# Latent attention: a list-scheduled order, masks of the maxima added by TensorE, single rows of maxima

## The chip, the cores and the metric

One core of one Trainium2 chip runs the kernel. The metric is the device time of the whole program in microseconds (us); the median of three runs of the kernel before is 1757.98 us. TensorE multiplies matrices into PSUM, VectorE (DVE) and ScalarE (ACT) read PSUM, GpSimd (POOL) works on SBUF alone, SyncE (SP) starts transfers.

## What is computed

A block of six layers over 2048 rows of 128 features: an expert layer with eight experts, windowed attention, the expert layer again, then a latent-attention block with four experts, a state-space layer, and the latent-attention block again. The change is in the latent attention, of which this is the core (16 heads of size 8, here over T = 2048 rows):

```python
scores = jnp.einsum('bhqd,bhkd->bhqk', q, k) / np.sqrt(HEAD_DIM)
causal = jnp.tril(jnp.ones((t, t), dtype=bool))
scores = jnp.where(causal, scores, -jnp.inf)
attn = jax.nn.softmax(scores, axis=-1)
out = jnp.einsum('bhqk,bhkd->bhqd', attn, v).transpose(0, 2, 1, 3).reshape(b, t, D_MODEL)
return out @ Wo.T
```

## The kernel before

`latent_attention` works in 16 units a stage, each of one group g of 512 query rows (four tiles of 128) and four heads; `ORDER` runs g = 0, 0, 1, 1, 2, 2, 3, 3, 3, 3, 2, 2, 1, 1, 0, 0. A unit has two passes.

The pass of maxima finds each query row's largest score. For each query tile, head and block of up to 512 keys, one item ("max", numbered m): TensorE puts 128 rows of scores into one of three PSUM banks (`maximum`, L1592; the contraction has 64 rows, so that two heads use the two row halves of the array), and VectorE takes the maximum over the columns. A unit has 16(g+1) items. Blocks left of the diagonal go through `tensor_reduce` (L1761). The block on the diagonal, 128 to 512 columns wide, needs the causal mask: `tensor_tensor_reduce` (L1766) adds the table `causal` (in SBUF, 512 columns of bf16) and reduces, and writes its sums to `masked`. At a unit's end VectorE joins the blocks' maxima (L1772) into `shift`, waits for that, and GpSimd (`chain_shift`, L1804 to L1807) writes it in three bf16 parts beside the queries, so that the second pass's scores come out less their maxima.

The pass of scores takes key tile after key tile (4(g+1) tiles, two halves of two heads each): TensorE makes transposed scores into a pair of banks (`score`, L1602, two pairs in turn), ScalarE takes the exponential of up to 1024 columns (L1709), GpSimd zeroes what lies above the diagonal in a unit's first four tiles (`cut_products`, L1826), and TensorE multiplies with the values (`weigh`, L1618, f32; a tile is weighed in two halves of 256 query rows). `plain` and `shift` are transposes of the unit's queries without and with the maxima (L1580) and their copies on ScalarE (L1714). `take` (L1734) and `out` (L1628, L1777, L1779) bring a unit's result back into rows. Beside them stand the output projection, the norm and routing of half of the rows (`mean`, `root`, `norm`, `turn`, `logits`, `place`; after `place` GpSimd issues eight indirect transfers, L545), in the first stage also 64 exponentials `power` (L1742) and four products `times_c` for the state-space layer.

All engines follow one list, `events`, made by `plan` before the program is built; each engine takes its own kinds of event from it, in order, and waits on semaphores. Before, a place is a number: item m of unit v stands at its index, the scores of a unit are spread evenly over the next unit's items behind a lead of 9, and everything else is set by an offset to these. Maxima stand in pairs, and TensorE waits once for both banks of a pair:

```python
if m % 2 == 0:
    bank_free(("max", (v, m + 1)))
```

## Time and profile before

| | us |
|---|---|
| median of three runs | 1757.98 |
| lowest, highest | 1755.60, 1759.52 |
| profiled execution | 1757.22 |
| its span | 1755.9 |
| busy: PE, DVE, ACT, POOL | 1238.1, 1196.7, 947.0, 570.0 |
| mean granted clock of TensorE, share of full | 0.834 |

A span is the time from the first to the last instruction. Busy time counts what an engine executes, not its waits; ends of matmuls are modelled. A row of the order of time gives the start, how long the instructions lasted, engine, line, operation, what is written and read with shapes (64*128 means 64 rows by 128 columns of the array), the count, and in brackets the idle time before it and what ended that. Neighbouring instructions overlap, so the distance from start to start is what one costs its engine. The clock is TensorE's, 1.00 for 2.4 GHz and 0.50 for 1.2 GHz.

### The profile page before, as it was taken

What the parts mean: (1) busy time and instruction counts of PE and PEld (TensorE: products, weight loads), DVE (VectorE), ACT (ScalarE), POOL (GpSimd) and SP (SyncE); (2) the same over time, 40 slices, a digit from 0 to 9 for tenths busy, and PEclk for the clock granted to TensorE, in tenths of its full rate; (3) what the DMA queues carried; (4) which work ended last, traced back from release to release, by engine and by line L of the source; (5) the groups of instructions that cost most, each with busy time, mean ns of one, the idle gap of its engine ahead of it and who ended that gap; (6) DMA issues with size and microseconds to landing.
All of it is one profiled execution on the core that took longest, in us unless ns stands there. A gap on an engine that the chain in (4) does not pass through costs nothing. (4 is left out here: it accounts for less than half of the span.)

```text
span 1755.9 us, 36353 instructions
## 1 busy us (share of the span) xinstructions
PE 1238.1 (71%) x13313; PEld 624.7 (36%) x13313; DVE 1196.7 (68%) x3279; ACT 947.0 (54%) x1500; POOL 570.0 (32%) x1032
## 2 busy tenths in 40 slices
PE   2754564366757788899886464776778898988746
PEld 2653453365532122222232453353222222223246
DVE  4358598436777899987862354277789999786234
ACT  0226774122445688888875240134557788887522
POOL 2331276146662411321123242275332111112323
PEclk9977675577577999999998695856799999999869
DMA  9410000021001100000000180000000000000012
GB/s 243 102 46 1 1 4 2 22 66 50 1 18 53 35 1 1 1 2 3 1 1 13 49 217 27 2 1 1 1 1 2 1 2 1 1 2 1 13 44 81
DMA packets 59137, 49.01 MB, mean 28 GB/s; under 512 B 7105, under 2 KB 54194, under 8 KB 58610
## 3 DMA queue, kind: packets, MB, share of 16 engines
q1 hardware_dynamic: 53282, 35.84, 7.9%
q0 software_dynamic: 4736, 9.74, 1.7%
q8 instruction: 109, 1.79, 0.4%
q10 hardware_dynamic: 944, 1.10, 0.2%
q14 instruction: 66, 0.54, 0.1%
HBM read 32.72 MB, written 18.38 MB: 29 GB/s over the span
## 5 line engine op out<-in xcount | busy, mean ns | idle before, releaser
L1709 ACT ACTIVATE arena<-psum 128x1024 f32<-128x1024 f32 (+3 forms) x640 | 561.0, 898 | 191.6 <-PE psum L1602 170.8
L1761 DVE TENSOR_REDUCE arena<-psum 128x1 f32<-128x512 f32 x768 | 479.8, 683 | 63.4 <-PE psum L1592 59.7
L1618 PE MATMUL psum<-arena 128*9 128x256 f32 (+2 forms) x4352 | 346.4, 394 | 0.9 <-POOL arena L1826 0.4
L1592 PE MATMUL psum<-arena 64*128 64x512 bf16 (+3 forms) x1280 | 240.2, 371 | 128.7 <-DVE arena L1761 58.3
L1766 DVE CUSTOM_DVE_ANT_0 arena<-psum,wqkv 128x384 bf16<-128x384 f32 (+3 forms) x512 | 230.3, 486 | 89.0 <-PE psum L1592 75.1
L1602 PE MATMUL psum<-arena 64*128 64x512 bf16 (+3 forms) x1280 | 233.7, 362 | 20.0 <-ACT arena L1709 15.0
L1826 POOL TENSOR_SCALAR_AFFINE_SELECT arena<-arena 128x256 f32<-128x256 f32 x256 | 103.6, 408 | 323.0 <-ACT arena L1709 320.4
L1592 PEld LDWEIGHTS psum<-arena 64*128 64x128 bf16 x1280 | 64.0, 94 | 383.2 <-DVE arena L1761 196.6
L1618 PEld LDWEIGHTS psum<-arena 128*9 128x9 f32 x4352 | 67.7, 89 | 174.3 <-issue 133.5
L1804 POOL CAST arena<-arena 128x16 bf16<-128x16 f32 x64 | 16.4, 257 | 327.7 <-DVE arena L1772 325.4
L677 DVE TENSOR_SCALAR small<-psum,YT 128x128 f32<-128x128 f32 x168 | 50.5, 342 | 78.0 <-PE psum L587 77.4
L632 ACT ACTIVATE small<-psum,YT 128x128 f32<-128x128 f32 x168 | 52.4, 364 | 83.5 <-PE psum L587 64.6
L587 PE MATMUL psum<-arena,YT 128*128 128x128 f32 x672 | 97.1, 292 | 0.1
L1602 PEld LDWEIGHTS psum<-arena 64*128 64x128 bf16 x1280 | 63.5, 95 | 93.1 <-ACT arena L1709 46.6
L1714 ACT ACTIVATE arena<-psum 128x1024 bf16<-128x1024 bf16 x64 | 65.5, 1023 | 52.3 <-PE psum L1580 48.3
L587 PEld LDWEIGHTS psum<-arena,YT 128*128 128x128 f32 x672 | 87.6, 204 | 2.9 <-issue 1.3
L578 PE MATMUL psum<-ident,ACCn 128*128 128x128 f32 x16 | 7.2, 470 | 90.7 <-DMA ACCn<-sorted_rows 58.1
L559 POOL DMA_INDIRECT made_rows<-arena,index x38 | 42.4, 1116 | 76.8 <-DVE arena L657 75.1
L545 POOL DMA_INDIRECT sorted_rows<-Yn,slot x32 | 31.4, 980 | 83.9 <-DVE slot L363 74.8
L597 PE MATMUL psum<-w,small 128*128 x304 | 43.0, 286 | 15.7 <-ACT small L632 12.7
L1580 PE MATMUL psum<-identb,arena 128*128 128x128 bf16 x512 | 44.5, 237 | 9.9 <-DVE psum L1750 3.9
L597 PE MATMUL psum<-big_w,small 128*128 x368 | 50.5, 281 | 0.6 <-issue 0.6
(353 smaller groups left out, 1962.9 us busy)
## 6 DMA issues: line engine op xcount, KB each, us to landing
arena<-taps SPq DMA_DIRECT2D x8, 1024.0 KB
big_w<-in_w SPq DMA_DIRECT2D x2, 2048.0 KB
ACCn<-made_rows SPq DMA_DIRECT2D x16, 256.0 KB, 3.6
regions<-sorted_rows SPq DMA_DIRECT2D x5, 741.8 KB, 4.6
sorted_rows<-arena SPq DMA_DIRECT2D x2, 1483.5 KB, 16.8
ACCn<-regions SPq DMA_DIRECT2D x32, 64.5 KB, 1.9
w<-in_w SPq DMA_DIRECT2D x2, 1024.0 KB
ACCn<-sorted_rows SPq DMA_DIRECT2D x6, 258.0 KB, 3.4
```

The source lines that it names most:

```text
L587: mm = pe.matmul(hidden_of(s, k), first[s % 2][:, k * P:(k + 1) * P], xt[s // GT % 2][:, (s % GT) * P:(s % GT + 1) * P], start=True, stop= ...
L597: mm = pe.matmul(psum[:, 4 + s % 2, 0:D], hid[s % 2][:, k, :], flat2[:, bass.ds(expert[s] * HID + k * P, D)], start=(k == 0), stop=(k == H ...
L632: half = act.activation(hid[s % 2][:, k, :], hidden_of(s, k), ACT.Relu, bias=first[s % 2][:, HID + k:HID + k + 1])
L677: half = dve.tensor_scalar(hid[s % 2][:, k, :], hidden_of(s, k), first[s % 2][:, HID + k:HID + k + 1], 0.0, ALU.add, ALU.max)
L1592: pe.matmul(psum[:, b, 0:w], plain_q[v % 2][rows, a, i * P:(i + 1) * P], keys[rows, 2 * hq + a, c * GW:c * GW + w], start=True, stop=True) ...
L1602: mm = pe.matmul(psum[:, b + r, off:GW], keys[rows, 2 * hq + a, t * P:(t + 1) * P], shift_q[v % 2][rows, a, off:GW], start=True, stop=True)
L1618: mm = pe.matmul(psum[32 * hh:32 * hh + 9, O_BANK, lo:hi], values[:, tile_of(v, j), 4 * hq + hh, :], prob[(t + hh // 2) % N_PROB][:, hh % ...
L1709: act.activation(prob[t % N_PROB][:, :, off:GW], both, ACT.Exp, scale=INV_SQRT_HD).then_inc(a_got, 1)
L1714: act.activation(dst, bank.bitcast(BF16).rearrange("p (a t) -> p a t", a=2), ACT.Copy).then_inc(a_got, 1)
L1761: dve.tensor_reduce(place, bank[:, 0:w], AX.X, ALU.max).then_inc(a_max_got, 1)
L1766: dve.tensor_tensor_reduce(out=masked[cuts % 2][:, 0:w], in0=bank[:, 0:w], in1=causal[:, GW - w:GW], scale=1.0, scalar=LEAST, op0=ALU.add, ...
L1826: pool.affine_select(out=part, in_=part, compare_op=ALU.is_ge, fill=0.0, base=0, pattern=[[0, 2], [1, P]], channel_multiplier=-1).then_inc ...
```

## The change

Four things change.

The order. `plan` no longer computes places but lists: it keeps a time at which each engine is free, by a table of costs, and emits whichever event of TensorE's could start soonest, ties by a rank. Items run ahead of the scores as banks come free. Events of the other engines are put into the list when their input is ready. A tile's two half weighings stand together. `power` is put wherever ScalarE would idle, and the products `scale` follow after each sixteenth.

Single rows. TensorE waits for one bank at each item instead of two banks at each pair.

The masks. A diagonal item is a matmul of the scores with start only, followed by a second matmul of `identb` with a 128-column bf16 table `causal` that adds -1e30 above the diagonal to the last 128 columns of the bank. VectorE's custom operation, its 512-column table and the two `masked` buffers are gone; all items are `tensor_reduce` (L1921 in the changed kernel).

The joining. A unit's maxima are joined after the first item of the next unit, not at its own end, without a wait behind; `row_max` has two buffers for that.

In the diff, cut to its core, "..." marks what is left out:

```diff
-LEAST = -3e38
...
-        causal = wqkv[:, D:3 * D].bitcast(BF16)
+        causal = wqkv[:, D:D + P // 2].bitcast(BF16)
...
-            places = []
-            start = [ITEMS_TO[v + 1] + LEAD for v in range(UNITS)] + [N_ITEMS + LEAD + 4 * TILES_OF[-1]]
-            half_at = [start[v] + (start[v + 1] - start[v]) * s / (2 * TILES_OF[v]) for v in range(UNITS) for s in range(2 * TILES_OF[v])]
-            half_at += [half_at[-1] + 2 * k for k in range(1, 24)]
-            for v in range(UNITS):
-                places += [(ITEMS_TO[v] + m - m % 2, "max", (v, m)) for m in range(4 * TILES_OF[v])]
-                places += [(ITEMS_TO[v] - 8 if v else -1, "plain", v), (start[v] - 3.1, "shift", v)]
-                places += [(half_at[2 * (TILES_TO[v] + j) + a] - 0.4, "score", (v, j, a)) for j in range(TILES_OF[v]) for a in range(2)]
-                for j in range(TILES_OF[v]):
...
+            free = {e: 0.0 for e in ("pe", "dve", "act", "pool")}
+            done, act_ring, dve_ring, weighed, later = {}, [], [], [], []
...
+            def put_act(kind, x, ready, pe_cost, cost):
+                p = run("pe", ready, pe_cost) + 0.15
+                while far and at["power"] < 64 and done.get(("score", (1, 0, 0))) and free["act"] + 0.2 < p + LAG:
+                    power(p)
+                emit(kind, x)
+                done[kind, x] = run("act", p + LAG, cost)
+                act_ring.append(done[kind, x])
...
+            def joined(v):
+                done["least", v] = run("dve", done.get(("chain", v - 1), 0.0) + LAG, 0.15)
+
+                def shifted(ready):
+                    done["chain", v] = run("pool", ready, 1.6)
+                put_off(done["least", v], "chain", v, shifted)
...
+                v, m = at["item"]
+                if v < UNITS and ("plain", v) in done:
+                    ready = done["plain", v] + LAG
+                    yield max(ready, ring_free(dve_ring, 3)), 6, "max", (v, m)
+                v, h = at["half"]
+                if v < UNITS and ("shift", v) in done and len(weighed) >= TILES_TO[v] + h // 2 - 2:
+                    yield max(done["shift", v] + LAG, ring_free(act_ring, 2)), 5, "score", (v, h // 2, h % 2)
+                v, j = at["weigh"]
...
+                v, j = at["weigh"]
+                if v < UNITS and ("score", (v, j, 1)) in done and (j or not v or ("take", v - 1) in done):
+                    ready = done["score", (v, j, 1)]
+                    if j < GT:
+                        ready = done.get(("cut", (v, j, 1)), 1e9)
+                    if j == 0 and v:
+                        ready = max(ready, done["take", v - 1])
+                    yield ready + LAG, 4, "weigh", (v, j)
...
+            while True:
+                options = [(max(free["pe"], ready), *rest) for ready, *rest in choices() if ready < 1e8]
+                if not options:
+                    if not later:
+                        break
+                    flush(min(entry[0] for entry in later))
+                    continue
+                soonest = min(options)[0]
+                if any(entry[0] <= soonest for entry in later):
+                    flush(soonest)
+                    continue
+                ready, _, kind, x = min((o for o in options if o[0] <= soonest + 0.05), key=lambda o: o[1])
+                if kind in ("plain", "shift"):
...
+                    put_dve(kind, x, ready, 0.22 * w / GW + (0.1 if c == ORDER[v][0] else 0.0), 0.067 + 0.533 * w / GW)
+                    at["item"] = (v, m + 1)
+                    if m + 1 == 4 * TILES_OF[v]:
+                        at["item"] = (v + 1, 0)
+                    if m == 0 and v:
+                        joined(v - 1)
+                    if at["item"] == (UNITS, 0):
+                        joined(v)
...
+                    put_act(kind, x, ready, 0.225 * w / GW, 0.19 + 1.66 * w / 1000)
...
+                    parts = [0.225 * (min(GW, k + GW // 2) - max(k, cut(v, j))) / (GW // 2) for k in (0, GW // 2) if cut(v, j) < k + GW // 2]
+                    for half in ((1,) if j == 0 else (0, 1)):
+                        emit(kind, (v, j, half))
+                    weighed.append(run("pe", ready, sum(parts)) + 0.16)
...
-                    if m % 2 == 0:
-                        bank_free(("max", (v, m + 1)))
-                    pe.matmul(psum[:, b, 0:w], plain_q[v % 2][rows, a, i * P:(i + 1) * P],
-                              keys[rows, 2 * hq + a, c * GW:c * GW + w], start=True, stop=True).then_inc(a_max_put, 1)
+                    bank_free(event)
+                    mm = pe.matmul(psum[:, b, 0:w], plain_q[v % 2][rows, a, i * P:(i + 1) * P],
+                                   keys[rows, 2 * hq + a, c * GW:c * GW + w], start=True, stop=(c < g))
+                    if c == g:
+                        mm = pe.matmul(psum[:, b, w - P:w], identb[:], causal, start=False, stop=True)
...
+                def joined(v):
+                    dve.wait_ge(a_max_got, dve_base + number["max", (v, 4 * TILES_OF[v] - 1)] + 1)
+                    if units + v:
+                        dve.wait_ge(a_chained, units + v)
+                    dve.tensor_reduce(shift, row_max[v % 2][:, :, 0:ORDER[v][0] + 1], AX.X, ALU.max, negate=True).then_inc(a_least, 1)
+
...
-                        place = row_max[:, i * 4 + hh, part:part + 1]
-                        if part < ORDER[v][0]:
-                            dve.tensor_reduce(place, bank[:, 0:w], AX.X, ALU.max).then_inc(a_max_got, 1)
-                        else:
-                            cuts += 1
-                            if cuts > 2:
-                                dve.wait_ge(a_max_got, dve_base + number[event] - 1)
-                            dve.tensor_tensor_reduce(out=masked[cuts % 2][:, 0:w], in0=bank[:, 0:w], in1=causal[:, GW - w:GW], scale=1.0,
-                                                     scalar=LEAST, op0=ALU.add, op1=ALU.max, accum_out=place).then_inc(a_max_got, 1)
-                        if m == 4 * TILES_OF[v] - 1:
-                            dve.wait_ge(a_max_got, dve_base + number[event] + 1)
-                            if units + v:
-                                dve.wait_ge(a_chained, units + v)
-                            dve.tensor_reduce(shift, row_max[:, :, 0:ORDER[v][0] + 1], AX.X, ALU.max, negate=True).then_inc(a_least, 1)
-                            dve.wait_ge(a_least, units + v + 1)
+                        dve.tensor_reduce(row_max[v % 2][:, i * 4 + hh, part:part + 1], bank[:, 0:w], AX.X, ALU.max).then_inc(a_max_got, 1)
+                        if m == 0 and v:
+                            joined(v - 1)
+                        if (v, m) == (UNITS - 1, 4 * TILES_OF[v] - 1):
+                            joined(v)
...
+                    elif kind == "scale":
+                        times_c(x)
```

In TensorE's order, in unit 8 of the first stage (g = 3), L1592 is an item, L1602 a half of a score tile, L1618 a half weighing. Before:

```order
985 L1592 MATMUL psum<-arena 128x512 x2
986 L1602 MATMUL psum<-arena 128x512 x2
987 L1618 MATMUL psum<-arena 9x256 x4
988 L1592 MATMUL psum<-arena 128x512 x2
989 L1602 MATMUL psum<-arena 128x512 x2
990 L1618 MATMUL psum<-arena 9x256 x4
991 L1592 MATMUL psum<-arena 128x384 x2
992 L1602 MATMUL psum<-arena 128x512 x2
993 L1618 MATMUL psum<-arena 9x256 x4
```

In the changed kernel, the same unit; L1745 is an item, L1748 a mask, L1758 a half of a score tile, L1774 a weighing:

```order
1137 L1758 MATMUL psum<-arena 128x512 x2
1138 L1745 MATMUL psum<-arena 128x512 x2
1139 L1774 MATMUL psum<-arena 9x256 x8
1140 L1758 MATMUL psum<-arena 128x512 x2
1141 L1745 MATMUL psum<-arena 128x384
1142 L1748 MATMUL psum<-wqkv,identb 128x128
1143 L1758 MATMUL psum<-arena 128x512 x2
1144 L1745 MATMUL psum<-arena 128x384
1145 L1748 MATMUL psum<-wqkv,identb 128x128
1146 L1745 MATMUL psum<-arena 128x512
1147 L1774 MATMUL psum<-arena 9x256 x8
```

Where each half tile had two items, a score and a half weighing, a tile now has its items in ones and twos between the scores and is weighed at once, and each diagonal item has a 128-column matmul behind it.

On GpSimd, near the end of the first stage, L1826 zeroes above the diagonal, L1804 to L1807 write a unit's maxima, and L545 is `place`'s eight indirect transfers. Before:

```order
351 L1807 CAST arena<-arena 128x4x4
352 L1826 AFFINE_SELECT arena<-arena 128x2x128
353 L545 DMA regions<-ACCn,slot 8576x129 x8
354 L1826 AFFINE_SELECT arena<-arena 128x2x128 x4
355 L1804 CAST arena<-arena 128x4x4
356 L1805 TENSOR_TENSOR arena<-arena 128x16
357 L1804 CAST arena<-arena 128x4x4
358 L1805 TENSOR_TENSOR arena<-arena 128x16
359 L1807 CAST arena<-arena 128x4x4
360 L1826 AFFINE_SELECT arena<-arena 128x2x128 x12
361 L545 DMA regions<-ACCn,slot 8576x129 x8
```

In the changed kernel the lines are L1978, L1956 to L1959 and L544:

```order
351 L1957 TENSOR_TENSOR arena<-arena 128x16
352 L1959 CAST arena<-arena 128x4x4
353 L544 DMA regions<-ACCn,slot 8576x129 x8
354 L1956 CAST arena<-arena 128x4x4
355 L1957 TENSOR_TENSOR arena<-arena 128x16
356 L1956 CAST arena<-arena 128x4x4
357 L1957 TENSOR_TENSOR arena<-arena 128x16
358 L1959 CAST arena<-arena 128x4x4
359 L1978 AFFINE_SELECT arena<-arena 128x2x128 x24
360 L544 DMA regions<-ACCn,slot 8576x129 x8
```

Sixteen cuts, those of the last two units, stood behind the first eight transfers; now it is twenty-four, those of the last three, and the last unit's maxima are written ahead of them.

## Rows read from the trace of the kernel before

**Rows 1.** The page: the span.
```profile
span 1755.9 us, 36353 instructions
```

**Rows 2.** Stretches, first stage: length, busy PE, PEld, DVE, ACT, POOL, then clock, DMA.
```profile
496.20:517.70 21.50, 13.43 (x80) 6.13 (x82) 14.81 (x66) 7.07 (x9) 10.29 (x29) 0.55 0.00 0
517.70:663.70 146.00, 114.19 (x1090) 32.34 (x1086) 127.55 (x320) 96.20 (x142) 46.06 (x129) 0.91 0.10 32
663.70:781.70 118.00, 105.13 (x1132) 26.53 (x1128) 110.93 (x250) 100.68 (x131) 28.74 (x47) 1.00 0.01 2
781.70:900.50 118.80, 107.12 (x1262) 34.48 (x1264) 92.69 (x239) 98.28 (x123) 17.91 (x52) 1.00 0.01 2
900.50:943.80 43.30, 33.50 (x310) 11.59 (x302) 19.79 (x91) 29.83 (x43) 15.09 (x30) 0.80 0.04 13
943.80:958.00 14.20, 10.26 (x114) 4.31 (x110) 1.79 (x5) 9.63 (x22) 5.98 (x17) 1.00 0.00 1
sum 461.80, PE 383.62 PEld 115.38 DVE 367.57 ACT 341.69 POOL 124.08; mean PE 63.94 PEld 19.23 DVE 61.26 ACT 56.95 POOL 20.68
```

**Rows 3.** The same, two stretches of the second stage.
```profile
1488.50:1603.50 115.00, 103.23 (x1137) 31.12 (x1136) 92.48 (x239) 95.95 (x119) 17.92 (x52) 1.00 0.01 1
...
1645.70:1663.00 17.30, 13.69 (x126) 4.79 (x118) 1.80 (x6) 10.13 (x23) 6.36 (x18) 0.80 0.00 1
```

**Rows 4.** The page, groups: busy, mean ns, idle before and who ended it.
```profile
L1761 DVE TENSOR_REDUCE arena<-psum 128x1 f32<-128x512 f32 x768 | 479.8, 683 | 63.4 <-PE psum L1592 59.7
...
L1766 DVE CUSTOM_DVE_ANT_0 arena<-psum,wqkv 128x384 bf16<-128x384 f32 (+3 forms) x512 | 230.3, 486 | 89.0 <-PE psum L1592 75.1
```

**Rows 5.** Order of time, TensorE, maxima of units 7 and 8 (start, us, what).
```profile
699.78 0.39 PE L1592 MATMUL psum<-arena 64*128 64x512 bf16 x2
700.00 0.38 PE L1602 MATMUL psum<-arena 64*128 64x512 bf16 x2
700.31 0.62 PE L1618 MATMUL psum<-arena 128*9 128x256 f32 x8
...
706.03 0.62 PE L1580 MATMUL psum<-identb,arena 128*128 128x128 bf16 x8
706.58 0.23 PE L1592 MATMUL psum<-arena 64*128 64x128 bf16 x2
...
706.99 0.62 PE L1618 MATMUL psum<-arena 128*9 128x256 f32 x8
707.54 0.39 PE L1592 MATMUL psum<-arena 64*128 64x512 bf16 x2
...
709.28 1.05 PE L1618 MATMUL psum<-arena 128*9 128x256 f32 x16
710.27 0.39 PE L1592 MATMUL psum<-arena 64*128 64x512 bf16 x2
```

**Rows 6.** Order of time, VectorE: a unit's end, and both kinds of maxima.
```profile
702.63 0.08 DVE L1766 DVE_READ_ACCUMULATOR2_ANT arena<- 128x1 f32 x1
...
703.00 3.68 DVE L1761 TENSOR_REDUCE arena<-psum 128x1 f32<-128x512 f32 x6
...
844.07 0.55 DVE L1766 CUSTOM_DVE_ANT_0 arena<-psum,wqkv 128x384 bf16<-128x384 f32 x1
...
844.63 2.48 DVE L1761 TENSOR_REDUCE arena<-psum 128x1 f32<-128x512 f32 x4
```

**Rows 7.** The end of the first stage: VectorE, TensorE, GpSimd, ScalarE.
```profile
936.95 0.56 DVE L1766 CUSTOM_DVE_ANT_0 arena<-psum,wqkv 128x384 bf16<-128x384 f32 x1 [6.03 <-remote]
...
937.57 0.50 PE L1592 MATMUL psum<-arena 64*128 64x384 bf16 x2 [4.07 <-issue]
...
935.99 0.95 POOL L545 DMA_INDIRECT regions<-ACCn,slot  x1 [0.31 <-issue]
...
922.96 3.98 ACT L1709 ACTIVATE arena<-psum 128x1024 f32<-128x1024 f32 x4 [3.06 <-PE psum L1602]
```

**Rows 8.** The powers on ScalarE, from 560 to 900 us.
```profile
L1742 ACT ACTIVATE big_w<-arena,logdt_pair 128x129 f32<-128x129 f32 x64 | 26.0, 406 | 0.0
```

172 lines of the change are left out of this document (129 added, 43 removed).

## The prediction

> **What bounds the kernel now.** I read the page first for the span, then the busy time by stretch, then the order of time of TensorE and VectorE, then the waits. The profiled execution took 1757.22 us, its span is 1755.9 us [rows 1], so 1.3 us lie around the span, and that execution is 0.8 us under the median of 1757.98. What I work out is a difference; I put it on the median.
>
> Latent attention runs twice, and the change touches nothing else: from 496.2 to 958.0 us [rows 2] and again until 1663.0 us [rows 3], some 461 us each, over half of the span. In the stretches the reader is to see that no engine idles much and that the bound wanders. Units 2 to 6 (517.7 to 663.7): VectorE is busy 127.6 of 146.0 us. Units 7 to 9: 110.9 of 118.0, with TensorE at 105.1. Units 10 to 13: TensorE 107.1 of 118.8 and VectorE only 92.7. Units 14 and 15: nobody, TensorE 33.5 and VectorE 19.8 of 43.3. Then 14.2 us of scores alone. VectorE's idle time before its two lines of maxima is 63.4 and 89.0 us over both stages, 59.7 and 75.1 of it for TensorE's L1592 [rows 4]: two engines that feed each other through three banks, each nearly full. So the question is what each needs in a stage and how much is lost in the coupling.
>
> **TensorE's prices, at full clock [rows 5].** Two maxima of 512 columns, on separate row halves, run side by side: the next 64-row work starts 0.22 us later (699.78 to 700.00). The score after them has the same columns but is followed by a weighing, and takes 0.31 (700.00 to 700.31): changing from 64-row matmuls to others costs 0.09. A half weighing takes 0.55 (706.99 to 707.54), a whole one 0.99 (709.28 to 710.27): the second half adds 0.44, so 0.11 is the change back. Eight transposes take 0.55 (706.03 to 706.58); less the change that is 0.055 each. The Trainium skill, page "TensorEngine Tiling (Array Packing)", section Key Properties, says that changing the tiling mode drains TensorE; the trace agrees, with 0.09 and 0.11 us. By that rule a full-array mask between 64-row matmuls drains the array twice, and the masks of a stage cost 256 x 0.25 = 64 us of TensorE; without it they would cost 14.
>
> **Masks on TensorE.** Per stage 256 matmuls (4 a tile, half of 512 masked maxima in both stages). Not in the trace; nearest row: a transpose of the same shape, 0.055. Lower bound 0.055 each (changes hidden), upper 0.055 + 0.09 + 0.11 = 0.25; I take the upper, since each mask stands between 64-row matmuls. Counting in the two orders, changes of shape go from about 607 to about 807 a stage: masks add some 420, and the list order takes some 220 away by weighing whole tiles. So +14 us (256 x 0.055) and +20 (200 x 0.10). A masked maximum no longer runs beside its partner: 128 pairs x 0.13 (mean 320 columns) = +17. Unmasked pairs that the new order separates, some 45 x 0.21 = +9. In sum **+60 us of TensorE's work a stage**: counted by these prices it is 331 before (maxima 58, scores 61, weighings 118, transposes and the rest 35, changes 60) and 391 after.
>
> **VectorE.** The second masked maximum of a pair, the custom operation over 384 columns with its read of the sum, holds VectorE for 0.56 us (844.07 to 844.63); four plain reductions of 512 columns last 2.48, 0.61 each, so 0.46 to 0.48 at 384 columns [rows 6]. I take 0.08 saved for each of 128 pairs, 10 us. A unit's end cost 0.37 us from the last read to the next reduction (702.63 to 703.00) [rows 6]; joined into the next row it is one reduction of about 0.2: 16 x 0.17 = 3 us. The joining's wait, now behind the next unit's first item, has one item behind it that TensorE covers with two full banks; GpSimd's writing starts some 0.6 us later, and the shift stands three and more items on, as before, so I cost it at nothing (0.5 us x 16 if it is waited for). VectorE falls from 367.6 us [rows 2] to about 354. ScalarE's work stays, 342 us [rows 2].
>
> **Where they stand, stretch by stretch,** TensorE's work at full clock (the prices over the order) against VectorE's, then what I take, with 3% on TensorE for what the prices leave out.
> - Units 0, 1 (21.5 us now): every maximum is masked, TensorE goes from 6 to 14 at full clock, but its clock here is 0.55 [rows 2]; VectorE 13. Waits, not work, fill this stretch now. I take 22: **+1**.
> - Units 2 to 6 (146.0): TensorE 92 to 121, VectorE 130 by its prices to 125. TensorE's clock is 0.91 now; with TensorE fuller it should fall less. 121 x 1.03 plus 5 for clock is 130, 6% for coupling: 138, **-8**.
> - Units 7 to 9 (118.0): TensorE 97 to 107, VectorE 113 to 110. A single row leaves two banks (1.2 us) of cover where a pair left one (0.6). 110 x 1.045 = 115, **-3**.
> - Units 10 to 13 (118.8, 115.0 in the second stage): TensorE 100 to 100, as whole weighings pay for the masks; VectorE 94 to 88. 103 x 1.05 = 108: **-11 and -7**.
> - Units 14, 15 (43.3): TensorE 25 now and after, more of the scores are put off. VectorE stands here 6.03 us with no releaser in the program, until GpSimd's eight scatters are over, the last at 935.99 + 0.95 [rows 7]; the next masked maximum starts as the last scatter ends, and TensorE waits with it, 4.07 us at 937.57. A reduction that reads PSUM alone may pass. 29: **-14**.
> - Scores behind the last maximum (14.2, 17.3): the order has three units left (24 cuts behind the scatters on GpSimd where 16 stood), not one and a half. ScalarE needs 29, a whole half tile 0.9 to 1.0 (four in 3.98, [rows 7]) and a cut one less, and 1.5 for gaps; the scatters, 8 x 1.26 (0.95 and 0.31 between them, [rows 7]) = 10.1 us, now hold back the first cuts of unit 13, some 6.5 us of it in the open, and 4 for the low clock that follows a stall. 41: **+27 and +24**.
> The sums are -8 and -7, with the head of the stage in each, where two rows of transposes now go ahead of the first maximum (+1 each: eight transposes, 0.55 at full clock, and the clock is 0.55 there [rows 2]). -15 + 2 = **-13 us: 1745.** The list order itself adds no work to other engines; the powers move forward on ScalarE and cost nothing there while it idles (50 of the 146 us of units 2 to 6, [rows 2]); without that cover they are 26 us [rows 8]. The four products on GpSimd come earlier; they delay cuts either way.
>
> **The rivals.**
> - *The changes of shape are mostly hidden and the cover works.* Masks at the lower bound give TensorE 40 us less; only the stretches where it is the bound gain, about 8 in units 2 to 6 and 4 in 10 to 13, and the coupling falls by a half per cent of 380: 14 less than the forecast in each stage, 1717. For it: in units 7 to 9 coupling already costs only 4%. Against: every change in the trace shows its 0.1 us.
> - *TensorE becomes the bound throughout* (slower). 391 x 1.03 = 403, plus 20 for low clock, is 423 of 461 us. If it still idles over 38 us a stage (it idles 78 now, [rows 2]), the stage is longer: single rows make TensorE stand at every bank while scores behind it are ready, in order. The forecast has 5% for coupling over the 380 us of units 2 to 13; at 10% each stage is 19 longer, 1783. It is slower than before from 6.7% on, where the 13 us are used up.
> - *The tail alone turns it* (slower): the stall behind the scatters drops the clock; in the stretch with such stops it is 0.80 on the mean, against 1.00 before and after [rows 2]. A tile of scores and weighing is 1.5 us of TensorE at full clock by the prices, 3.0 at half, where ScalarE needs 1.8: 1.2 more on ten of the sixteen tiles, +12 in each stage beyond the forecast, 1769.
> - *Nothing*: gains in the body equal the tail, 1758. That the change doesn't do what it says is excluded by the order.
> A page's rule bears on the last maxima: the Trainium skill, "SBUF — State Buffer", section Who interferes with whom, says that tensor_reduce never contends with GpSimd for the shared port on trn2; no row here shows a reduction during scatters.
>
> **How the numbers follow.** Forecast (1735 to 1754) 0.30; hidden changes 0.20; nothing 0.13; TensorE bound 0.22; tail 0.15. A measurement can tell 0.2%, 3.5 us, from no change. Faster 0.50, same 0.13, slower 0.37. The range leaves out a tenth on each side: low end 1708, the fast rival with 5 us more a stage; high end 1795, where TensorE's bound and half of the tail meet. The likeliest case's own range is 1735 to 1754. Unknown costs widen both ways: the mask between 0.055 and 0.25, the coupling between 3 and 10%.
>
> **What would show it.** TensorE's busy time in 517 to 900 us near 90% or more, with gaps of 0.09 to 0.11 around each 128-column mask; VectorE no longer stopped by scatters; the last maximum 30 us before the stage's last exponential, or more, where it is 14 now; the exponentials of unit 13 stopped once for 5 to 8 us behind GpSimd. Wrong would be: masks spaced at 0.06, a tail under 30 us, or a stage in which VectorE, not TensorE, is the fuller engine in units 2 to 6.

## The result and the profile after

The changed kernel takes 1860.03 us (median of 4 runs, 1857.84 to 1865.88) where the kernel before took 1758.75 us on the same chip: a ratio of 1.058, 95% interval 1.056 to 1.061. It is slower by about 101 us. The forecast was 1745, its range 1708 to 1795.

Words used below: an item is one block of maxima (a matmul and its reduction), a half weighing is the product of one key tile's exponentials with the values for 256 of the unit's 512 query rows, a whole weighing is both halves in a row. Coupling is what a stretch takes beyond the work of its busier engine. A stretch is cut at VectorE's maxima, so the scores and weighings in it need not belong to the same units.

Below are the page's span, the stretches of the first stage (length, busy PE, PEld, DVE, ACT, POOL, clock, DMA; they answer [rows 1] and [rows 2]) and the groups of maxima and masks that answer [rows 4]. L1921 is a reduction, L1745 an item, L1748 a mask.

```profile
span 1856.6 us, 36344 instructions
```
```profile
517.60:682.40 164.80, 148.96 (x1360) 56.62 (x1357) 126.77 (x242) 112.18 (x182) 62.30 (x141) 0.92 0.09 29
682.40:816.10 133.70, 121.82 (x1186) 41.67 (x1185) 112.48 (x200) 93.48 (x106) 13.27 (x39) 0.98 0.01 1
816.10:932.40 116.30, 107.31 (x1063) 40.50 (x1062) 91.04 (x173) 84.10 (x105) 16.17 (x48) 1.00 0.01 1
932.40:963.60 31.20, 29.80 (x242) 14.27 (x243) 19.34 (x57) 18.15 (x29) 5.41 (x16) 0.84 0.01 1
963.60:1007.10 43.50, 27.56 (x276) 9.11 (x272) 2.52 (x8) 27.01 (x45) 16.50 (x35) 0.84 0.04 13
```
```profile
L1921 DVE TENSOR_REDUCE arena<-psum 128x1 f32<-128x512 f32 (+3 forms) x1280 | 707.9, 605 | 193.9 <-PE psum L1748 94.1
...
L1745 PE MATMUL psum<-arena 64*128 64x512 bf16 (+3 forms) x1280 | 382.4, 370 | 52.7 <-DVE arena L1921 46.8
...
L1748 PE MATMUL psum<-wqkv,identb 128*128 128x128 bf16 x512 | 123.5, 241 | 0.0
```

In units 2 to 6 TensorE is now busy 149.0 of 164.8 us where it was 114.2 of 146.0 [rows 2]; in units 7 to 9 121.8 of 133.7 where it was 105.1 of 118.0. VectorE's busy time has not changed (710.1 us in the two groups of [rows 4], 707.9 now), but the idle time before its maxima went from 152.4 to 193.9 us in both stages together. The same stretches for both stages, in us, of the kernels that the argument uses (what each is stands below):

| kernel | 0-1 | 2-6 | 7-9 | 10-13 | 14-15 | scores behind last maximum | stages 1 / 2 |
|---|---|---|---|---|---|---|---|
| before | 21.5 / 22.5 | 146.0 / 146.2 | 118.1 / 118.1 | 118.8 / 114.9 | 42.9 / 41.9 | 13.9 / 16.5 | 461 / 460 |
| forecast | 22 | 138 | 115 | 108 | 29 | 41 | 453 |
| after | 21.6 / 22.3 | 164.6 / 163.2 | 133.8 / 133.8 | 116.4 / 116.4 | 31.1 / 31.1 | 43.5 / 43.6 | 511 / 510 |
| after, no masks | 14.7 / 14.7 | 161.4 / 159.3 | 134.5 / 132.2 | 110.8 / 112.4 | 27.5 / 26.2 | 43.8 / 43.8 | 493 / 489 |
| old order, joined, single rows, no masks | 21.1 / 22.1 | 140.9 / 140.6 | 116.2 / 116.2 | 118.3 / 113.2 | 40.7 / 41.9 | 16.8 / 16.1 | 454 / 450 |

The last column tells where the time went: +50 us in each stage, nothing elsewhere. In spans, the old order with everything else but the masks takes 1733.7, list order without masks 1816.6, with masks 1856.6: **the list order costs 83 us, the masks 40, and single rows with the joining and without VectorE's masks give 22 back.** The 83 is a lower bound: the run with the old order contains a stop of some 6 us a stage that is not the order's doing (last section); by the ratios, 1.040 against 0.988, the order costs 91 us.

TensorE in order of time, unit 8, with one reduction row of VectorE; it answers [rows 5] and [rows 6]. L1758 is a score, L1774 a weighing.

```profile
740.13 0.28 PE L1745 MATMUL psum<-arena 64*128 64x256 bf16 x1
740.35 0.23 PE L1748 MATMUL psum<-wqkv,identb 128*128 128x128 bf16 x1
740.51 0.28 PE L1745 MATMUL psum<-arena 64*128 64x256 bf16 x1
740.72 0.23 PE L1748 MATMUL psum<-wqkv,identb 128*128 128x128 bf16 x1
740.88 0.39 PE L1758 MATMUL psum<-arena 64*128 64x512 bf16 x2
...
742.45 0.39 PE L1758 MATMUL psum<-arena 64*128 64x512 bf16 x2
...
743.84 0.39 PE L1745 MATMUL psum<-arena 64*128 64x512 bf16 x1 [0.35 <-DVE arena L1921]
744.15 1.05 PE L1774 MATMUL psum<-arena 128*9 128x256 f32 x16
745.14 0.39 PE L1758 MATMUL psum<-arena 64*128 64x512 bf16 x2
```
```profile
743.09 2.48 DVE L1921 TENSOR_REDUCE arena<-psum 128x1 f32<-128x512 f32 x4 [0.28 <-PE psum L1745]
```

A mask takes 0.16 us and the item before it 0.21 to 0.22, some 0.37 together. A pair of 512 columns took 0.22 [rows 5], so one item of 256 columns in a pair would take 0.055; 0.31 more is the price, 0.25 for the mask with its changes and 0.06 for the lost partner. The Trainium skill, "TensorEngine Tiling (Array Packing)", section Key Properties, has the drain at a change of mode; these rows agree with it. From score to score (742.45 to 745.14) a tile with four unmasked items takes 2.69 us. VectorE's row of four lasts 2.48, with 0.28 of idle time ahead of it: neither engine is full, and a weighing of 0.99 (744.15 to 745.14) stands between the items.

The end of the first stage answers [rows 7]: GpSimd's first scatter, VectorE's last two maxima, and the exponentials behind.

```profile
961.95 1.09 POOL L544 DMA_INDIRECT regions<-ACCn,slot  x1 [16.48 <-DVE slot L429]
```
```profile
962.28 1.29 DVE L1921 TENSOR_REDUCE arena<-psum 128x1 f32<-128x512 f32 x2 [0.92 <-PE psum L1748]
```
```profile
976.60 1.09 ACT L1865 ACTIVATE arena<-psum 128x512 f32<-128x512 f32 x2 [8.73 <-PE psum L1758]
```

The last two maxima run beside the first scatter and end at 963.57, so no later scatter meets one; ScalarE stands once for 8.73 us. The powers of [rows 8] now all stand in units 2 to 6:

```profile
L1898 ACT ACTIVATE big_w<-arena,logdt_pair 128x129 f32<-128x129 f32 x64 | 20.1, 400 | 0.0
```

### The profile page after: what moved, and what is told of

Read it like the earlier page. It is cut to its first block and busy times, and to the rows that moved or that the text cites. A ratio compares the mean times of both kernels' runs of the same rounds, so it can differ in the third digit from the quotient of the medians.

```text
span 1856.6 us, 36344 instructions
## 1 busy us (share of the span) xinstructions
PE 1393.0 (75%) x13825; PEld 740.4 (40%) x13825; DVE 1197.3 (64%) x2767; ACT 938.9 (51%) x1500; POOL 566.7 (31%) x1032
## 5 line engine op out<-in xcount | busy, mean ns | idle before, releaser
L1921 DVE TENSOR_REDUCE arena<-psum 128x1 f32<-128x512 f32 (+3 forms) x1280 | 707.9, 605 | 193.9 <-PE psum L1748 94.1
L1865 ACT ACTIVATE arena<-psum 128x1024 f32<-128x1024 f32 (+3 forms) x640 | 541.8, 895 | 241.3 <-PE psum L1758 240.2
L1745 PE MATMUL psum<-arena 64*128 64x512 bf16 (+3 forms) x1280 | 382.4, 370 | 52.7 <-DVE arena L1921 46.8
L1774 PE MATMUL psum<-arena 128*9 128x256 f32 (+2 forms) x4352 | 311.0, 399 | 30.8 <-issue 15.3
L1758 PE MATMUL psum<-arena 64*128 64x512 bf16 (+3 forms) x1280 | 235.2, 359 | 15.4 <-ACT arena L1865 13.9
L1978 POOL TENSOR_SCALAR_AFFINE_SELECT arena<-arena 128x256 f32<-128x256 f32 x256 | 101.8, 406 | 292.4 <-ACT arena L1865 289.7
L1745 PEld LDWEIGHTS psum<-arena 64*128 64x128 bf16 x1280 | 106.0, 95 | 207.9 <-DVE arena L1921 158.8
L1956 POOL CAST arena<-arena 128x16 bf16<-128x16 f32 x64 | 16.3, 254 | 434.8 <-DVE arena L1911 432.7
L1774 PEld LDWEIGHTS psum<-arena 128*9 128x9 f32 x4352 | 90.8, 92 | 139.5 <-ACT arena L1865 45.9
L1758 PEld LDWEIGHTS psum<-arena 64*128 64x128 bf16 x1280 | 59.8, 94 | 175.7 <-ACT arena L1865 112.8
L1748 PE MATMUL psum<-wqkv,identb 128*128 128x128 bf16 x512 | 123.5, 241 | 0.0
L1748 PEld LDWEIGHTS psum<-wqkv,identb 128*128 128x128 bf16 x512 | 50.0, 98 | 125.6 <-issue 111.3
L1929 DVE RECIPROCAL arena<-psum 128x16 f32<-128x16 f32 x32 | 8.1, 254 | 88.4 <-PE psum L1784 88.3
L544 POOL DMA_INDIRECT sorted_rows<-Yn,slot x32 | 31.2, 975 | 82.7 <-DVE slot L362 73.5
## 6 DMA issues: line engine op xcount, KB each, us to landing
big_w<-in_w SPq DMA_DIRECT2D x2, 2048.0 KB, 21.6
```

The source lines that it names most:

```text
L1745: mm = pe.matmul(psum[:, b, 0:w], plain_q[v % 2][rows, a, i * P:(i + 1) * P], keys[rows, 2 * hq + a, c * GW:c * GW + w], start=True, stop= ...
L1748: mm = pe.matmul(psum[:, b, w - P:w], identb[:], causal, start=False, stop=True)
L1758: mm = pe.matmul(psum[:, b + r, off:GW], keys[rows, 2 * hq + a, t * P:(t + 1) * P], shift_q[v % 2][rows, a, off:GW], start=True, stop=True)
L1774: mm = pe.matmul(psum[32 * hh:32 * hh + 9, O_BANK, lo:hi], values[:, tile_of(v, j), 4 * hq + hh, :], prob[(t + hh // 2) % N_PROB][:, hh % ...
L1865: act.activation(prob[t % N_PROB][:, :, off:GW], both, ACT.Exp, scale=INV_SQRT_HD).then_inc(a_got, 1)
L1921: dve.tensor_reduce(row_max[v % 2][:, i * 4 + hh, part:part + 1], bank[:, 0:w], AX.X, ALU.max).then_inc(a_max_got, 1)
```

## The experiments

Times are medians; ratios are to the kernel before, run beside each, with 95% intervals.

**1. The parts of the change, one at a time.** Masks back on VectorE in the changed kernel:

```diff
-                    if c == g:
-                        mm = pe.matmul(psum[:, b, w - P:w], identb[:], causal, start=False, stop=True)
...
+                            dve.tensor_tensor_reduce(out=masked[cuts % 2][:, 0:w], in0=bank[:, 0:w], in1=causal[:, GW - w:GW], scale=1.0,
+                                                     scalar=LEAST, op0=ALU.add, op1=ALU.max, accum_out=place).then_inc(a_max_got, 1)
```

> The changed kernel (1860 us) with its masks given back to VectorE's custom operation; order, single rows and joining stay. If the masks' 64 us of TensorE a stage are the cause (theory masks), two stages give back nearly all: 1750 to 1775. If it is the order and the rows of one, which let TensorE stand at each bank (theory rows: an unmasked maximum takes 0.27 us of TensorE's time in unit 8 where it took 0.11), only what masks cost beyond cover comes back: 1800 to 1830. If the scores put off behind the last maximum are the cause (theory tail, 43.5 us where 14 stood), 1830 or more.

1818.19 us, 1.041 (1.039 to 1.042): the range of theory rows.

The old order with its masks on TensorE, put into the kernel before:

```diff
+                    if c == g:
+                        mm = pe.matmul(psum[:, b, w - P:w], identb[:], causal, start=False, stop=True)
...
-                        if part < ORDER[v][0]:
+                        dve.tensor_reduce(row_max[:, i * 4 + hh, part:part + 1], bank[:, 0:w], AX.X, ALU.max).then_inc(a_max_got, 1)
```

> The kernel before (1758 us) with only its masks moved to TensorE, the order of before and pairs of banks kept. Theory masks: TensorE's slack of units 0 to 9 takes a part, units 10 to 15 nothing: 30 to 50 us a stage, 1820 to 1860. Theory rows and theory tail: the masks find cover, 1765 to 1790.

1842.79 us, 1.055 (1.053 to 1.057): the range of theory masks.

The kernel before with single rows alone:

```diff
-                    if m % 2 == 0:
-                        bank_free(("max", (v, m + 1)))
+                    bank_free(event)
```

> The kernel before with one wait for one bank at each maximum instead of one for both banks of a pair; order and masks of before. Theory rows: maxima no longer run side by side where VectorE is the bound, TensorE stands 0.6 us between the two with its scores behind it: 20 to 50 us slower, 1780 to 1810. Theory masks and tail: 1750 to 1762.

1735.95 us, 0.994 (0.992 to 0.995): faster by 10 us, under one per cent, and outside both ranges. Theory rows had this run 20 to 50 us slower, so it falls, although its ranges fit the runs with the new order: what they lose comes from the order itself.

The changed kernel without its mask matmuls (the two lines with - of the first diff), and so without the mask of the maxima:

> The changed kernel with the mask matmuls left out: the maxima are taken over the unmasked diagonal blocks (the exponentials are still cut by GpSimd). It takes all of the masks' price away and leaves order, rows and joining. Theory masks: 1735 to 1760, a little under the run with masks on VectorE. Theory rows: 1790 to 1820. Theory tail: 1825 or more.

1817.88 us, 1.040 (1.038 to 1.042). What follows: on VectorE the masks cost this order nothing (1818.19 against 1817.88); on TensorE they cost 40 us of span. The other 3.5 to 4 per cent come with the order, since single rows alone cost nothing.

**2. The old order without masks,** single rows, plain reductions on the diagonal:

```diff
-                    if m % 2 == 0:
-                        bank_free(("max", (v, m + 1)))
+                    bank_free(event)
...
-                        if part < ORDER[v][0]:
+                        dve.tensor_reduce(row_max[:, i * 4 + hh, part:part + 1], bank[:, 0:w], AX.X, ALU.max).then_inc(a_max_got, 1)
```

> The kernel before with a wait for one bank at each item and with plain reductions on the diagonal (left out: the causal mask of the maxima; the exponentials are still cut, so a row's shift is the maximum over later keys too). No mask on any engine. The single rows alone gave 1736 us. Theory (VectorE is the bound of units 2 to 9 and the scatters stop the custom operation alone): VectorE has some 10 us a stage less to do and is not stopped in units 14 and 15, 1715 to 1730 us. Rival (TensorE's own chain sets the pace there): 1732 to 1738 us.

1741.18 us, 0.990 (0.987 to 0.993): neither the 1715 to 1730 of less work on VectorE nor the rival's 1732 to 1738. The kernel before took 1757.94 us beside it and 1746.25 beside the single rows alone, so the ratios are the fairer comparison: 0.990 against 0.994. With the joining too (only the order now differs from the changed kernel without masks):

```diff
+                        if m == 0 and v:
+                            joined(v - 1)
+                        if (v, m) == (UNITS - 1, 4 * TILES_OF[v] - 1):
+                            joined(v)
```

> The same as the kernel before with single rows and plain reductions without masks, and in addition a unit's maxima joined behind the first item of the next unit, as in the changed kernel. Against the changed kernel without its mask matmuls (1818 us) only the order of events differs. Theory: the join costs nothing or gains 2 to 6 us (16 x 0.17 a stage) against the run without it, and the list order alone costs 85 to 100 us. Rival (the later join holds back the shift and so the next unit's scores): 4 us or more slower than without the joining.

1735.74 us, 0.988 (0.984 to 0.992). The two cannot be told apart; the order alone costs 83 us of span, a little under the 85 to 100 expected. The old order with masks on TensorE (and the pairs of before) took 1842.79 us where the kernel before took 1746.25 beside it, 97 us more or 0.19 us for each of 512 masks; in units 0 to 13 of both stages its trace is 97.5 us longer than that of the first of these two runs, 0.22 for each of 448 masks. Units 7 to 9 and 10 to 13, without masks and then with them:

```profile
655.70:772.60 116.90, 111.78 (x1138) 32.06 (x1130) 110.13 (x201) 100.44 (x132) 28.66 (x47) 1.00 0.01 2
772.60:890.60 118.00, 110.82 (x1264) 36.43 (x1256) 91.54 (x175) 98.29 (x123) 17.85 (x52) 1.00 0.01 2
```
```profile
684.50:812.80 128.30, 119.61 (x1182) 34.64 (x1178) 112.75 (x202) 101.84 (x131) 28.73 (x48) 1.00 0.01 1
812.80:944.80 132.00, 125.86 (x1322) 44.66 (x1320) 93.73 (x175) 99.13 (x122) 17.94 (x53) 1.00 0.01 2
```

48 masks lengthen units 7 to 9 by 11.4 us, 0.24 each; by the prices they are 15 us with the lost partners, so three quarters of it is in the open, though by the forecast's sum VectorE had more to do there. Masked items come two in a row. From one reduction's start to the next VectorE takes 0.47 us without masks and 0.68 with them, on the mean over 45 items on the diagonal in units 7 to 9 (a unit's last is left out), while the others stay at 0.65.

**3. First theory on the order: scores catch up and stop at unit starts.** In the changed kernel without masks the gaps between one unit's last exponential and the next one's first sum to 50 us a stage; before, they sum to 10. So the scores were held to the old pace, and then the maxima too (both without masks):

```diff
-                if v < UNITS and ("shift", v) in done and len(weighed) >= TILES_TO[v] + h // 2 - 2:
+                at_item = 4 * TILES_TO[at["item"][0]] + at["item"][1]
+                if v < UNITS and ("shift", v) in done and len(weighed) >= TILES_TO[v] + h // 2 - 2 and (
+                        at["item"][0] == UNITS or at_item >= half_at(v, h) - 1):
```

> The changed kernel without mask matmuls, with a score allowed only when the maxima stand where the kernel before had it (nine items into the next unit, then evenly). Theory bubble: no stop at unit starts, units 2 to 9 fall from 295 to 262 to 270 us a stage; the tail of some 44 us stays: 1750 to 1770. Theory block: 1800 to 1815, as the whole weighings stay.

1811.19 us, 1.036 (1.034 to 1.038).

```diff
-                if v < UNITS and ("plain", v) in done:
+                if v < UNITS and ("plain", v) in done and (
+                        at["half"][0] == UNITS or 4 * TILES_TO[v] + m <= half_at(*at["half"]) + 3):
```

> As the paced one, and the maxima may not run over three items ahead of the same pace, so that 14 halves are left behind the last maximum, as before (13), not 34. Theory bubble: units 2 to 9 as in the paced kernel, and the tail is 14 to 18 us for 20 to 25 more in units 10 to 15: within 10 us of the paced one, 1740 to 1765. Theory block: 1800 to 1815. If the tail is what the put-off scores cost by the scatters and the low clock, it is 10 to 15 us faster than the paced one.

1828.86 us, 1.047 (1.045 to 1.049). The gaps went to 13 and 9 us, the time stayed: the gaps were a sign that the rest was slow, not its cause. The theory fell: both runs missed its ranges, 1750 to 1770 and 1740 to 1765. The planner's prices, set to what the trace shows (a tile's weighing from 0.45 to 0.98 us among them), did not help either:

```diff
...
-                    parts = [0.225 * (min(GW, k + GW // 2)
+                    parts = [0.49 * (min(GW, k + GW // 2)
...
```

> The changed kernel without mask matmuls, its planner's prices set to what the trace shows: a half of a score tile 0.27, a whole weighing 0.98, a maximum 0.16 us of TensorE. If wrong prices are the cause (theory prices), the order comes out near the best of the list rule: 1740 to 1770. Theory bubble: scores still run as early as they can and still stop at each unit's start; only the scores left behind the last maximum fall from 32 to 19 halves, which other stretches pay for: 1795 to 1820. Theory block: the same as bubble.

1852.57 us, 1.060 (1.058 to 1.062), 35 us slower than with the old prices. (Both lines go on alike behind what is shown; the prices of a score and of an item were changed too.)

**4. Second theory: the whole weighing is a block.** Without masks, the second half weighing moved behind the next item in the finished list (k runs over `events`, near are the next items):

```diff
+                if kind == "weigh" and x[2] == 1 and 0 < x[1] < TILES_OF[x[0]] - 1 and events[k - 1] == ("weigh", (x[0], x[1], 0)):
...
+                        events.insert(near[0] + 1, events[k])
+                        del events[k]
```

> The changed kernel without mask matmuls (1818 us, 72 over the kernel before) with a tile's second half weighing put behind the next maximum. Theory block: a whole weighing and a score, 1.2 us of TensorE without an item, outlast what single rows leave VectorE in two banks; units 2 to 9 fall from 295 to some 265 us a stage, 1755 to 1770. Theory bubble: the list lets the scores catch up with the maxima, so that each unit begins with 6 to 13 us without a score and its scores are then crowded; the weighings' place changes little: 1800 to 1820.

1778.84 us, 1.017 (1.015 to 1.019): 39 us back, units 7 to 9 from 134.5 to 124.2. And from the other side, halves joined in the old order (single rows, no masks):

```diff
-                        places += [(half_at[step] + 0.6, "weigh", (v, j, 0))]
+                        places += [(half_at[step + (0 < j < TILES_OF[v] - 1)] + 0.6, "weigh", (v, j, 0))]
```

> The kernel before with single rows and plain reductions without masks, and the two half weighings of a tile together, at the place of the second, as the changed kernel has them; all else of the old order stands. Theory 1 (a whole weighing is a block of 1.0 us in which VectorE runs out of filled banks): units 7 to 9 take 5 to 10 us a stage more than with halves apart, the kernel 20 to 40 us more. Rival (fewer changes of shape on TensorE pay for the block, and the loss of the list order lies elsewhere): within 5 us of the run with halves apart, or faster.

1783.75 us, 1.014 (1.010 to 1.017), 43 us over the same with halves apart. TensorE's items in units 7 to 9, halves apart and then whole (behind the second bar: idle time before them, and who ended it):

```profile
L1591 PE MATMUL psum<-arena 64*128 64x512 bf16 (+3 forms) x192 | 46.7, 366 | 5.1 <-DVE arena L1757 4.4
```
```profile
L1591 PE MATMUL psum<-arena 64*128 64x512 bf16 (+3 forms) x192 | 53.2, 365 | 15.3 <-DVE arena L1757 14.8
```

The stretch went from 116.9 to 126.8 us, and the waits for a bank grew by 10.4. Two full banks cover VectorE for 1.2 us; score, whole weighing and next item take 0.31 + 0.99 + 0.22 = 1.52. VectorE runs dry behind each block, and the lost time is not made up, for TensorE then waits in order for its banks. The block's price is shown from both sides: 39 us back when it is split, 43 lost when it is made.

**5. Third theory: the weighing also stands too close to its scores.** Scores and maxima paced and halves apart, the edits of 3 and 4 together, should have been the old order but for trifles:

> The changed kernel without its mask matmuls (left out: the causal mask of the maxima; the exponentials are still cut), scores and maxima held to the pace of the order before, and the second half weighing put behind the next maximum. What is left of the list order is small. Theory 1 (the loss of the list order is the whole weighing, a block of 1.0 us that TensorE does between two items): units 7 to 9 take 117 to 121 us a stage and the kernel 1740 to 1770 us. Rival (the loss lies in something else that all list orders share, such as where plain and shift rows, powers or joins stand): units 7 to 9 stay at 124 us or more and the kernel stands at 1785 us or more.

1813.50 us, 1.031 (1.028 to 1.035): a miss. Its weighings in units 7 to 9, behind the second bar their waits:

```profile
L1787 PE MATMUL psum<-arena 128*9 128x256 f32 (+2 forms) x692 | 52.7, 381 | 14.1 <-ACT arena L1878 13.9
```

TensorE waits there for the exponential. In the old order two halves of scores lie between a tile's second scores and its weighing (45 of 48 tiles in units 7 to 9); in the list order one for 33 of 48 tiles, none for 3 and two for 11. Three kernels test that, the first in the old order by its table of places, the others by one condition more for a weighing:

```diff
-                    step = 2 * (TILES_TO[v] + j) + (4 if j == 0 else 3)
+                    step = 2 * (TILES_TO[v] + j) + (4 if j == 0 else 2)
```
```diff
-                if v < UNITS and ("score", (v, j, 1)) in done and (j or not v or ("take", v - 1) in done):
+                if v < UNITS and ("score", (v, j, 1)) in done and (j or not v or ("take", v - 1) in done) and (
+                        j + 1 == TILES_OF[v] or ("score", (v, j + 1, 1)) in done):
```

> The kernel before with single rows and plain reductions (left out: the causal mask of the maxima; the exponentials are still cut), and each tile's two half weighings half a tile earlier: one half of scores lies between a tile's second scores and its weighing, as in the list order, where two lay. Theory (TensorE then waits in order for the exponential, with items queued behind): waits for ScalarE ahead of the weighings in units 7 to 9 rise from 0 to 5 us or more, the kernel stands 15 to 40 us above the 1741 us of the run without the shift. Rival (scores spread evenly leave 1.3 us, enough for one exponential of 1.0): within 5 us of 1741.

1757.06 us, 1.005 (1.003 to 1.007), 16 us over the run without the shift, and more than that by the edit: the earlier run had the stop behind the scatters (below), and this one, 7 us shorter in units 14 and 15, had not. Units 0 to 13 of both stages are 32 us longer, and the ratios, 1.005 against 0.990, differ by 26 us. Units 7 to 9 went from 116.9 to 122.5 and units 2 to 6 from 139.6 to 149.4; waits for ScalarE ahead of weighings in units 7 to 9 were 3.1 us, under the 5 expected.

> The changed kernel without its mask matmuls (left out: the causal mask of the maxima), scores and maxima paced, half weighings apart (1813 us, with 13.9 us of waits for the exponential ahead of the weighings of units 7 to 9), and now a tile is weighed only behind the second scores of the next tile. Theory 2 (what is left of the list order's loss is the distance from score to weighing): those waits go under 2 us, units 7 to 9 take 117 to 122 us instead of 134.8, the kernel 1750 to 1775 us. Rival (another cause common to all list orders): 1790 us or more.

1788.68 us, 1.023 (1.021 to 1.026): above the theory's 1775 and just under the rival's 1790. In units 7 to 9 the theory holds to the number: 134.8 to 120.6 us, with 0.4 us of waits:

```profile
L1788 PE MATMUL psum<-arena 128*9 128x256 f32 (+2 forms) x688 | 52.5, 381 | 0.4 <-ACT arena L1904 0.4
```

The whole kernel gained 25 us, not the 38 to 63 expected: units 2 to 6 stayed at 167 and 153 us.

> The changed kernel without its mask matmuls (left out: the causal mask of the maxima), its list order unpaced, with the half weighings apart (1779 us) and behind the next tile's second scores. Theory: block and distance are all that is wrong in units 7 to 13; 7 to 9 take 117 to 121 us where 124 stood, the kernel 1745 to 1768 us. Rival (the block alone counted here, the scores ran ahead and hid the distance): 1775 to 1785 us.

1766.77 us, 1.011 (1.009 to 1.013): 12 us under halves apart alone and within the expected total, but in the wrong place: units 7 to 9 did not move (124.5), the gain is in 10 to 15, less 4 to 6 us a stage in the scores behind the last maximum. So block and distance explain some 47 of the order's 83 us (spans 1816.6 and 1769.1). The other 35 stay open. In units 2 to 6 this kernel takes 160.4 and 153.3 us in the two stages where the old order takes 140.9 and 140.6, in units 7 to 9 124.5 and 124.0 where that takes 116.2. Two things that the traces show were not tried apart. The list order does more in units 2 to 6: 624 weighing and 190 score matmuls for 576 and 178, and in the first stage also the 128 matmuls of the state-space layer, which the old order has in units 10 to 13. And the granted clock is lower, 0.86 and 0.89 for 0.92 in units 2 to 6, 0.95 for 1.00 in units 7 to 9 of the first stage.

**6. The same in the changed kernel, masks included:**

> The changed kernel whole, its masks on TensorE included, with the half weighings apart and behind the next tile's second scores; nothing is left out. Theory: the same gain as without masks, minus what more changes of shape cost beside the masks, 1785 to 1815 us against 1860. Rival (with the masks TensorE is so full that the extra changes of shape eat the gain): 1830 us or more.

1847.45 us, 1.055 (1.051 to 1.059). The rival was right: of some 50 us that the same edit gives without masks, 8 are left by the spans (1856.6 and 1848.3) and 13 by the medians; the intervals of the two ratios, 1.056 to 1.061 and 1.051 to 1.059, overlap. Units 7 to 9:

```profile
681.60:816.50 134.90, 130.20 (x1185) 38.59 (x1185) 112.85 (x200) 93.86 (x106) 13.36 (x39) 0.94 0.01 1
```

TensorE is busy 130.2 of 134.9 us. The same kernel without masks takes 124.5 there, so 48 masks cost 10.4 us, 0.22 each, where they cost nothing in the changed kernel (133.8 with, 134.5 without): once the waits are mended, the masks fill the room again. That TensorE's work is the bound here fits both numbers; no run has tested it.

**7. Which engine was the bound before?** Every reduction reads only half of its columns, in the old order with single rows and without masks; TensorE's work is whole. Against that kernel (experiment 2) the edit is:

```diff
-dve.tensor_reduce(row_max[:, i * 4 + hh, part:part + 1], bank[:, 0:w], AX.X, ALU.max)
+dve.tensor_reduce(row_max[:, i * 4 + hh, part:part + 1], bank[:, 0:w // 2], AX.X, ALU.max)
```

> The kernel before with single rows and plain reductions without masks (1741 us), where each reduction reads only the first half of its columns (left out: the mask of the maxima and half of the scores that they are taken over; TensorE does all of its work). VectorE's work falls by about 40%. If VectorE bounds units 2 to 9, as the forecast had it, units 7 to 9 fall from 116.9 to about 102 us, TensorE's 97 of the prices and 5%, and the kernel to 1680 us or less. If TensorE's own chain of instructions is the bound there, units 7 to 9 stay at 110 us or more and the kernel at 1715 us or more.

1645.23 us, 0.942 (0.939 to 0.945). Units 2 to 6, 7 to 9, 10 to 13 and two neighbouring items, a half tile apart:

```profile
515.10:630.90 115.80, 109.18 (x1090) 34.24 (x1094) 77.70 (x240) 94.54 (x143) 46.40 (x131) 1.00 0.12 40
630.90:738.40 107.50, 104.63 (x1131) 28.75 (x1130) 69.06 (x202) 99.30 (x133) 28.79 (x48) 1.00 0.01 2
738.40:849.40 111.00, 106.80 (x1262) 34.79 (x1262) 57.50 (x175) 97.23 (x123) 17.94 (x53) 1.00 0.01 2
```
```profile
690.97 0.39 PE L1591 MATMUL psum<-arena 64*128 64x512 bf16 x2
691.19 0.38 PE L1601 MATMUL psum<-arena 64*128 64x512 bf16 x2
...
691.50 0.62 PE L1617 MATMUL psum<-arena 128*9 128x256 f32 x8
692.05 0.34 PE L1591 MATMUL psum<-arena 64*128 64x384 bf16 x2
```

VectorE's work did set the time of units 2 to 9, as forecast: the three stretches were 139.6, 116.9 and 118.0 us. But with half of it gone they still take 116, 107.5 and 111 us, where TensorE's prices said 92, 97 and 100 and the expectation 102 for the middle one. A half tile undisturbed takes what they say: 0.22 + 0.31 + 0.55 = 1.08, and 690.97 to 692.05 is 1.08. So does the sum: with each kind of matmul at the shortest distance to its follower that these traces have, units 7 to 9 come to some 97 to 98 us (an estimate from all start times). Of the other 9 or 10 us some 3 are waits that end with a ScalarE instruction, which is now busy 99.3 of 107.5 us, and 3 to 4 lie where the two matmuls of a pair do not run side by side, as in a score that takes 0.53 for 0.31 (643.83 to 644.36):

```profile
643.83 0.60 PE L1601 MATMUL psum<-arena 64*128 64x512 bf16 x2
644.36 0.62 PE L1617 MATMUL psum<-arena 128*9 128x256 f32 x8
...
662.34 0.39 PE L1601 MATMUL psum<-arena 64*128 64x512 bf16 x2 [0.42 <-ACT arena L1708]
```

So TensorE is busy 97% of the 107.5 us, but this run does not show that it alone needs them all.

**8. The best version:** single rows and the joining, with masks, order and half weighings of before (a second `row_max` is the only new buffer):

> The kernel before with single rows (1736 us when alone, ratio 0.9935) and the joining of a unit's maxima into the next unit's row; masks, order and half weighings as before, nothing is left out. Theory (VectorE's work at a unit's end stood in the open): 2 to 6 us less than with single rows alone, ratio 0.990 to 0.993. Rival (TensorE's chain sets the pace, VectorE's work is hidden): the same as with single rows alone, 0.993 to 0.996.

1728.23 us, 0.987 (0.985 to 0.990), where the kernel before took 1748.75 beside it: 21 us faster, and by the ratios 7% faster than the changed kernel, with nothing left out. That is more than either side expected. By the ratios the joining gives some 0.6% over single rows alone, which ran on another chip; by the spans (1729.7 and 1731.8) 2 us. How much of it is the joining's stays open. Neither span may be set against the 1755.9 us of the kernel before: 12 to 14 us of that difference stand in units 14 and 15, where its trace has the stop behind the scatters and theirs have not.

## Why the prediction was wrong

*Prices.* Mask 0.25, changes of shape, weighings: right, with rows. VectorE's 13 us a stage less: wrong in the changed kernel, where the groups fell by 2.2 us in both stages together (710.1 to 707.9). The custom operation was priced about right: in the old order without masks the same maxima take 688.5 us. But reductions that follow one another overlap, and waiting for a mask they stand alone more often: in the list order they take 693.7 us without masks and 707.9 with them.

*The step that failed: from TensorE's prices to the length of a stretch ("what I take, with 3% on TensorE for what the prices leave out", and 5 to 6% of coupling on that).* The forecast added 17, 8 and 8 us to TensorE's 121, 107 and 100 (138, 115, 108). Measured are 164.8, 133.7 and 116.3 us: 44, 27 and 16 more than the prices. The rows ahead of the prediction had the warning. Before, the prices gave 92, 97 and 100 us for stretches of 146.0, 118.0 and 118.8, which is 54, 21 and 19 us more, and [rows 2] show TensorE busy 114.2, 105.1 and 107.1, 24, 8 and 7% over the prices where the forecast had 3%. With these ratios 121, 107 and 100 become 150, 116 and 107; measured busy times are 149.0, 121.8 and 107.3.

That agreement is a rule of thumb and partly luck, for busy time is not work alone. In units 2 to 6 the clock of 0.91 is in it, which the forecast had already charged with 5 us. And short waits hide under the modelled ends of matmuls. Unit 8 before:

```profile
739.77 0.62 PE L1618 MATMUL psum<-arena 128*9 128x256 f32 x8
740.42 0.39 PE L1592 MATMUL psum<-arena 64*128 64x512 bf16 x2
...
740.96 0.62 PE L1618 MATMUL psum<-arena 128*9 128x256 f32 x8
741.72 0.39 PE L1592 MATMUL psum<-arena 64*128 64x512 bf16 x2
```

The items start 0.65 and 0.76 us behind a half weighing that costs 0.55 [rows 5], and no idle time is told. Over units 7 to 9 before, the distances from start to start exceed the shortest ones by some 20 us (an estimate as above), 19 of them ahead of items, most of which start 0.06 us behind the end of a VectorE instruction; told as idle before items are 12.9. The same sum of shortest distances gives some 128, 114 and 100 us for the changed kernel's stretches, against prices of 121, 107 and 100. So the prices of TensorE's work were short by at most 7 us a stretch, and what lies above the work, 37, 19 and 16 us where the forecast had 17, 8 and 8, was the larger part of the miss. Nor does TensorE's work alone bound units 7 to 9 of the changed kernel: with its 48 masks taken away the stretch stays (133.8 and 134.5).

*What the waits were, first: the block.* Coupling stood at 4.5 to 6%; TensorE idled 9.6, 8.9 and 7.7% in the three stretches, hidden waits not counted. "A single row leaves two banks (1.2 us) of cover where a pair left one" was set against one item, not against what stands in front of it in the new order, 1.52 us with the whole weighing. The order rows ahead of the prediction show eight matmuls of it in a row. The halves apart and the halves joined price the block at 39 and 43 us. The distance from scores to weighing adds 10 to 12 us (spans 1779.2 and 1769.1, medians 1778.84 and 1766.77); the rest of the order's loss is open.

*Second: work averaged over a stretch.* In units 7 to 9 TensorE's 107 stood against VectorE's 110, so VectorE was to hide the masks. In the old order three quarters of their price showed there. Masked items come two together, and three banks do not carry that over. In the list order, where TensorE waited anyway, they cost 0.08 each (40 us for 512): nothing in units 7 to 9, 3 to 6 us a stage in each of units 2 to 6, 10 to 13, and 14 and 15, and 7 us in units 0 and 1, which I had put down to waits.

*"The list order takes some 220 changes away"* was about right (from 569 to 356 in the traces of the two orders without masks) and worthless: changes saved by whole weighings were paid for by the block. I had costed the order as a gain of 20 us of TensorE a stage; it cost some 40 us of time.

*The end of the stage.* 41 us of scores behind the last maximum: 43.5. Stop of the exponentials 5 to 8: 8.73. Units 14 and 15 at 29: 31.1. All near, but one reason was wrong: plain reductions do not always pass the scatters (last section); here only two maxima were left when these began. Units 10 to 13 at 108: 116.4, the coupling again. Head: +1 forecast, 0 measured. *Powers at nothing:* right here, where units 2 to 6 of the first stage are 1.4 us longer than of the second; in the paced order it is 13.7 us (167.0 and 153.3). The 128 matmuls of the state-space layer stand in the same stretch of the first stage in both of these kernels, so neither number is of the powers alone.

*The rivals.* "TensorE becomes the bound throughout", at 0.22, came nearest. Its mechanism was right in one half, the coupling of 10% from single items in order, and not in the other: taking the masks, 64 us of TensorE a stage by the prices, out of the changed kernel gives back 20 us a stage. Its price, 1783, was too low by the same step. Worked out afterwards, with 10% of coupling and the busy ratios of before, it gives (150 + 116 + 107) / 0.9 = 414 us for units 2 to 13, where the forecast had 138 + 115 + 108 = 361 and 414.8 was measured: 53 us a stage more, 1851. That is a fit to the result, not a forecast.

*The signs.* Those named for the forecast all came: TensorE 91% busy from units 2 to 13, the fuller engine in units 2 to 6, masks spaced 0.16 behind 0.22, a tail over 30 us, one stop of the exponentials (8.73 us for 5 to 8). The time was 115 us off all the same, so the signs could not tell the forecast from this rival.
